# Correlation and mixing with 32x32 blocks: four tiles of the PE array in place of block-diagonal 128x128 operands

## The reference, cut to what matters

```python
x = x + xattn(layernorm(x), ctx, ctx, Wq, bq, Wk, bk, Wv, bv, Wo, bo)
x = x + ffn(layernorm(x), W_in, b_in, W_out, b_out)

# xattn
qf = jnp.fft.rfft(qt)
kf = jnp.fft.rfft(kt)
c = qf.real * kf.real + 1j * -(qf.imag * kf.imag)
corr = jnp.fft.irfft(c, n=Lq)
mean_value = jnp.mean(corr, axis=(1, 2))           # over heads and channels: 2048 delays
weights, delay = jax.lax.top_k(mean_value, top_k)  # top_k = int(2 * ln 2048) = 15
tmp_corr = softmax(weights)
out = sum_k tmp_corr[k] * roll(v, -delay[k])       # then out @ Wo + bo
```

## Time and profile before

| | |
|---|---|
| median of 3 runs | 185.46 us (182.85 to 186.11) |
| the profiled execution | 184.77 us, of it 183.0 us from the first to the last instruction |
| TensorE, DVE, ACT, GpSimd busy | 164.3, 129.0, 123.8, 30.3 us |
| from the first GR matmul to the first TR matmul | 39.87 to 91.32 us |
| granted TensorE clock, mean | 0.986 of 2.4 GHz |

### The profile page before, as it was taken

One profiled execution on the slowest core, in us unless ns is written; L12 is line 12 of the kernel. 1 busy time (PEld: TensorE's weight loads), 2 busy tenths in 40 slices (PEclk: granted clock), 3 DMA queues, 4 the chain that ended last, 5 costly groups with the idle time before them and its releaser, 6 DMA issues.

```text
span 183.0 us, 2815 instructions
## 1 busy us (share of the span) xinstructions
PE 164.3 (90%) x1054; PEld 120.7 (66%) x1054; DVE 129.0 (70%) x262; ACT 123.8 (68%) x203; POOL 30.3 (17%) x47
## 2 busy tenths in 40 slices
PE   7599999989997949999899967899999979999991
PEld 5499444979965626999756655444444547888880
DVE  1006697936456657973349978699997779999964
ACT  3254347766666993134653999999898849999910
POOL 5004000300003000000005820006920005212000
PEclk9999999999999996999999999999999999999998
DMA  4999998000000000000000000000000000001316
GB/s 142 262 290 407 441 351 274 3 0 4 2 0 4 0 0 0 0 0 0 0 4 0 2 4 0 0 0 0 4 2 0 0 0 4 0 0 61 134 38 229
DMA packets 6268, 12.17 MB, mean 66 GB/s; under 512 B 576, under 2 KB 4032, under 8 KB 6128
## 3 DMA queue, kind: packets, MB, share of 16 engines
q1 hardware_dynamic: 6112, 11.99, 19.2%
q10 hardware_dynamic: 144, 0.01, 0.1%
HBM read 9.90 MB, written 2.10 MB: 66 GB/s over the span
## 4 chain that ended last, share of the span: by engine, by line
PE 70%; ACT 14%; DVE 7%; DMA 4%; issue 3%; SPq 1%; DVEq 0%
PE ps L1184 13%; PE ps L968 8%; PE ps L1152 7%; PE ps L1157 7%; PE ps L958 6%; PE ps L991 4%; PE ps L1083 4%; PE ps L980 4%; DMA arena<-ctx_in_dram 4%; ACT arena L534 3%; PE ps L929 3%; PE ps L1097 3%; PE ps L1003 2%; PE ps L1072 2%; PE ps L1092 2%
## 5 line engine op out<-in xcount | busy, mean ns | idle before, releaser
L1184 PE MATMUL ps<-woutq,arena 128*128 128x256 f16 x256 | 28.7, 273 | 1.3 <-ACT arena L587 0.7
L1184 PEld LDWEIGHTS ps<-woutq,arena 128*128 128x128 f16 x256 | 24.7, 98 | 5.4 <-ACT arena L587 1.5
L572 ACT ACTIVATE arena<-ps,colv,sm 128x512 f32<-128x512 f32 x32 | 23.7, 783 | 2.0 <-PE ps L1157 0.5
L881 DVE SCALAR_TENSOR_TENSOR arena<-scr,sm,arena 128x1024 f16<-128x1024 int16 x16 | 21.3, 1373 | 0.0
L860 DVE TENSOR_REDUCE sm<-arena 128x1 f32<-128x1024 f32 (+1 forms) x17 | 18.9, 1148 | 2.5 <-ACT arena L572 2.5
L1152 PE MATMUL ps<-arena,winq 128*128 128x512 bf16 x64 | 18.6, 379 | 0.3 <-ACT arena L564 0.3
L1157 PE MATMUL ps<-arena,winq 128*128 128x512 bf16 x64 | 18.6, 379 | 0.0
L587 ACT ACTIVATE arena<-arena,sm 128x1024 f16<-128x1024 f32 x15 | 16.5, 1136 | 0.0
L958 PE MATMUL ps<-wvo,arena 128*128 128x256 f32 x64 | 16.3, 408 | 0.0
L958 PEld LDWEIGHTS ps<-wvo,arena 128*128 128x128 f32 x64 | 12.7, 205 | 3.2 <-issue 1.5
L968 PE MATMUL ps<-arena,wqk 128*128 128x512 f32 x32 | 14.0, 595 | 0.0
(11 more groups left out here) (215 smaller groups left out, 299.2 us busy)
## 6 DMA issues: line engine op xcount, KB each, us to landing
tabs<-tab_dram SPq DMA_DIRECT2D x1, 2416.0 KB, 17.0
arena<-x_dram SPq DMA_DIRECT2D x4, 512.0 KB, 9.2
out_dram<-arena SPq DMA_DIRECT2D x8, 256.0 KB, 2.1
arena<-ctx_in_dram SPq DMA_DIRECT2D x3, 448.0 KB, 7.9
arena<-winT_dram SPq DMA_DIRECT2D x1, 1024.0 KB, 18.4
arena<-wout_dram SPq DMA_DIRECT2D x1, 1024.0 KB, 19.6
arena<-ctx_in_dram SPq DMA_DIRECT2D x2, 224.0 KB, 3.1
arena<-wqT_dram SPq DMA_DIRECT2D x1, 256.0 KB, 8.5
```

What stands on the lines that cost most here:

```text
L572: a.activation(H[:, f, 512 * c:512 * c + 512], bank("M1", n), ACT.Gelu, bias=colv[:, 6 + f:7 + f], scale=sc1[:, f:f + 1]).then_inc(S["h_re ...
L881: v.scalar_tensor_tensor(out=part, in0=scr16[:, n % 4, :], scalar=rf[:, f:f + 1], in1=piece(Hhi, n), op0=ALU.mult, op1=ALU.subtract).then_ ...
L1184: return t.matmul(o[k // 2][:, 256 * (k % 2):256 * (k % 2) + 256], part[:, t0:t0 + 128], woutq[:, f, :], start=start, stop=stop)
```

## The change

- Every product of 32x32 blocks becomes four matmuls, one for each bin j of the group, with operands and result on 32 rows each (`quadrants`). BU, BUT and NM_ go, with the copies that filled them (L447, L486, L507, L756) and the memsets.
- GR: 4 matmuls with 32 weight columns and 32 moving columns, over all 128 channel rows, for each old one of 128 by 128; the result is already in row form, in 2 units, one emptied by ACT and one by DVE.
- UU: UT by `gram`, 32x32 each. IN: the sum over the frequency parts is done by 64 matmuls of 32x32 against P, with the factors in column 0 of `blocks`; the DVE steps L697, L701 and L703 go. ME and TM change places.
- Weights: W1 is transposed, SE (8 matmuls) puts the result onto rows, RR (64 matmuls of 32x32 by 1 column) replaces W2 and the products and sums on DVE. DVE then only scales a table XY (2 instructions), and MX is 128 matmuls of 32x32, two tables summed in PSUM.
- MIX is in row form (512 columns instead of 2048), OO is 128 matmuls with 32 rows, 128 weight columns and 32 moving columns. They rotate through four banks, and the four units of a channel half end together. The rank of the units changes: ACT has the units of j = 0 and 2, DVE those of 1 and 3, so ACT now adds both constants.
- VP is 16 units of one group instead of 8 of two; the exponentials no longer stand behind BUT copies and part of the quantisation on ACT; two of the four XD units of DVE go to ACT, and the reduction of wout on DVE comes ahead of GR.

The core of the diff:

```diff
             def gramian(i):
-                pe.wait_ge(S["qt_ready"], 5 + i)
                 o = take_bank(pe, "GR", i)
-                for m in range(4):
-                    g = 4 * i + m
+                for m in range(8):
                     for k in range(2):
-                        c0 = 2048 * k + 128 * g
-                        last = t.matmul(o[:, 128 * m:128 * m + 128], qt[:, c0:c0 + 128], xt[:, c0:c0 + 128],
-                                        start=(k == 0), stop=(k == 1))
...
+                        for j, q in quadrants():
+                            c0 = 2048 * k + 128 * (8 * i + m) + 32 * j
+                            last = t.matmul(o[q, 32 * m:32 * m + 32], qt[:, c0:c0 + 32], xt[:, c0:c0 + 32],
+                                            start=(k == 0), stop=(k == 1))
...
-                for g in range(4 * i, 4 * i + 4):
-                    last = t.matmul(bank("UU", 0)[:, 32 * g:32 * g + 32], BU[:, g, :], gram[:, g, :], start=True, stop=True)
+                pe.wait_ge(S["gram_d" if i else "gram_a"], 1)
+                for g in range(8 * i, 8 * i + 8):
+                    for j, q in quadrants():
+                        last = t.matmul(bank("UU", 0)[q, 32 * g:32 * g + 32], tb3("UT")[q, g, :], gram[q, g, :], start=True, stop=True)
...
-            done(t.matmul(o[0:NS, :], tb("J"), pr2.rearrange("p g c -> p (g c)"), start=True, stop=True))
+            for g in range(NG):
+                for j, q in quadrants():
+                    last = t.matmul(o[q, 0:NM], blocks[q, 32 * g:32 * g + 32], tb3("P")[q, g, :], start=(g == 0), stop=(g == NG - 1))
+            done(last)
...
+            pe.wait_ge(S["wT_ready"], 1)
+            o = take_bank(pe, "RR", 0)
+            for g in range(NG):
+                for j, q in quadrants():
+                    last = t.matmul(o[q, g:g + 1], tb3("UT")[q, g, :], wT[q, g:g + 1], start=True, stop=True)
+            done(last)
+            vproj(10, 11, 12)
+            for h in range(2):
+                pe.wait_ge(S["xy_ready"], h + 1)
+                o = take_bank(pe, "MX", h)
+                for m in range(8):
+                    for n in range(2):
+                        for j, q in quadrants():
+                            last = t.matmul(o[q, 32 * m:32 * m + 32], tb3("USW" if n else "U")[q, 8 * h + m, :], xy[q, n, 8 * h + m, :],
+                                            start=(n == 0), stop=(n == 1))
+                done(last)
+            vproj(13, 14, 15)
+            pe.wait_ge(S["mix_a"], 1)
+            pe.wait_ge(S["mix_d"], 1)
+            pe.wait_ge(S["vh_ready"], NG)
+            for h in range(2):
+                o = [take_bank(pe, "OO", 4 * h + j) for j in range(NJ)]
+                for g in range(NG):
+                    for j, q in quadrants():
+                        last = t.matmul(o[j][:, 32 * g:32 * g + 32], xh[q, 256 * g + 128 * h:256 * g + 128 * h + 128], MIX[q, g, :],
                                         start=True, stop=True)
-                    done(last)
+                        if g == NG - 1:
+                            done(last)
```

More of the change, by code:

```diff
@@ L58, in shape_tables @@
     P = V * (sign / D)[:, :, None, None]
[L59 to L63, removed]
+    USW, X, Y = U.copy(), V.copy(), np.zeros_like(V)
+    for m in range(0, NM, 2):
+        USW[:, m], USW[:, m + 1] = U[:, m + 1], U[:, m]
+        X[:, m + 1] = V[:, m]
+        Y[:, m], Y[:, m + 1] = V[:, m + 1], -V[:, m + 1]
+    X[0, 1], Y[0, 0:2] = V[0, 1], 0
     rows = [AF + 1 if x < TC - AF * NB else AF for x in range(NB)]
@@ L113, in build @@
         xt = slot(3)
[L114 to L117, removed]
+        blocks = slot(4, 528)
+        MIX = slot(4, 512, 1024).rearrange("p (g c) -> p g c", g=NG)
         ct = slot(5)
@@ L174, in build @@
         warm = small(2)
-        ab, mean, ex, wn, eq, pre, gone = (small(16) for _ in range(7))
-        negmx, zr, rz, eqrow, neq = (small(1) for _ in range(5))
+        mean, ex, wn, eq, pre, tie, eqe, top, wT = (small(16) for _ in range(9))
+        negmx, zr, rz, eqrow, neq, thr = (small(1) for _ in range(6))
         m16 = small(16, NB)
@@ L670, in _ @@
             v.tensor_scalar(ss1, ss1, 127.0, None, ALU.mult).then_inc(S["ss1_ready"], 1)
-            for k in range(1, 8, 2):
+            for k in XD_DVE:
                 filled(dve, "XD", k)
@@ L704, in _ @@
-            filled(dve, "ME", 0)
-            v.tensor_copy(mean, bank("ME", 0)[:, 0:NB]).then_inc(S["mean_ready"], 1)
+            v.tensor_copy(ins[:], bank("IN", 0)[:, 0:NM]).then_inc(S["ins_ready"], 1)
             filled(dve, "TM", 0)
@@ L776, in _ @@
+            vproj(10, 11, 12)
+            filled(dve, "MX", 1)
+            v.tensor_copy(MIX[:, 8:16, :], bank("MX", 1)[:, 0:256].rearrange("p (g c) -> p g c", g=8)).then_inc(S["mix_d"], 1)
+            vproj(13, 14, 15)
+            for u in range(1, 8, 2):
+                filled(dve, "OO", u)
+                v.tensor_copy(spectrum(u), bank("OO", u).rearrange("p (g b r) -> p g b r", g=NG, b=NB)).then_inc(S["os_d"], 1)
             y3 = yn.rearrange("p (b d) -> p b d", b=NB)
@@ L1057, in _ @@
             done(last)
-            pe.wait_ge(S["w1_ready"], 1)
-            o = take_bank(pe, "W2", 0)
-            done(t.matmul(o, tb("JT", NS), own, start=True, stop=True))
-            vproj(3)
-            vproj(4)
-            vproj(5)
-            def mix(*units):
-                for i in units:
-                    pe.wait_ge(S["nm_ready"], i // 2 + 1)
-                    pe.wait_ge(S["nm_a"], i // 2 + 1)
-                    o = take_bank(pe, "MX", i)
-                    for m in range(4):
-                        g = 4 * i + m
-                        last = t.matmul(o[:, 128 * m:128 * m + 128], BUT[:, g, :], NM_[:, g, :], start=True, stop=True)
-                    done(last)
@@ L1075, in attend @@
-            def attend(*units):
-                for i in units:
-                    q, h = i // 2, i % 2
-                    pe.wait_ge(S["vh_ready"], 2 * q + 2)
-                    pe.wait_ge(S["mix_ready"], q + 1)
-                    o = take_bank(pe, "OO", i)
-                    for m in range(4):
-                        g = 4 * q + m
-                        last = t.matmul(o[:, 128 * m:128 * m + 128], xh[:, 256 * g + 128 * h:256 * g + 128 * h + 128], MIX[:, g, :],
+            vproj(9)
```

324 lines of the change are left out of this document (128 added, 196 removed).

## The result

The changed kernel is no faster. Its median is 186.48 us (185.93 to 187.49, 4 runs) against 185.79 (182.85 to 186.72) of the kernel before on the same chip; the ratio is 1.0152, interval 1.0094 to 1.021, so by the ratio a slowdown of about 1.5%. The prediction took 2% for the bound of no change. The profiled execution takes 185.93 us with a span of 183.9 (before 184.77 and 183.0).

What follows compares the result with a forecast made beforehand. TensorE (busy 90%) was taken to bound most of the 51.45 us stage, chains of short steps the rest; -5.8 - 0.6 - 1.3 - 0.4 + 0.8 + 0.9 = -6.4 gave 178.4 us, 8-in-10 range 171 to 211.3.

Steps and rivals of the forecast that it cites:

- p: Pace per pair (weight load plus matmul) in GR, UU, IN, RR, MX; taken as 16 ns, 1 ns being 0.90 us.
- o: Pace per pair in OO, with 128 weight columns, over 256 pairs; taken as 28 ns, 111 without overlap.
- (a): GR and UU, before 12.07 us: 390 pairs would take 6.2 us at p = 16; -5.8 us.
- (b): UU to the first maximum, before 6.29 us: DVE steps go, but WVO, IN and BVO stand on the path; -0.6 us.
- (c): Maxima to wn, before 8.65 us: exponentials no longer wait for BUT copies and table load; wn after 7.35 us; -1.3 us.
- (d): wn to the first TR matmul, before 24.45 us: would take 24.1, including 1.7 gained by full clock; -0.4 us.
- (e): ACT loads the Sqrt table after its last OO copy, delaying the first TR copy; +0.8 us.
- (f): Changes of the array's shape lose about 0.1 us each, at some 12 borders instead of some 5; +0.9 us.
- case 2: Issue floor near 26 ns shared by all tiles, or little overlap: p 19 to 29, 181 to 190 us; chance 0.24.
- Case 4: Tile changes cost about 0.1 us, or clock falls to 1.2 GHz; 215 us with all pairs at 50 ns; chance 0.14.
- cases 1 and 4: The first: tiles overlap, p 7 to 19, 170 to 181 us, chance 0.42; the other is Case 4.
- case 3: Weight loads do not overlap between tiles: OO takes 28.4 us instead of 7.2; 199.6 to 211.3 us; chance 0.2.

Runs made afterwards that it cites:

- j_major: The changed kernel with the loop over the four tiles outermost in GR and OO, so only one tile works at a time; 225.19 us.
- oo_cols128: The changed kernel with 128 moving columns instead of 32 in every OO matmul (OO's values are then others); 182.98 us.
- hybrid: The changed kernel with GR and OO block-diagonal as before the change and VP units 13 to 15 between the MX units; 175.98 us, ratio 0.950.
- gr_block: The changed kernel with GR alone put back to 128 by 128 matmuls with diagonal copies; ratio 0.9979 to the kernel before, profiled execution 183.65 us.
- hybrid_oo_tiles: hybrid with OO alone back in tiles, with its MIX copies and owners of units; ratio 0.9961, profiled execution 184.2 us.

## Why the prediction failed

The forecast was 178.4 us, faster; it came out at 186.48, within 2% on the slow side. The unknown on which it hung most went its way, even further than forecast: p is 8.6 ns and not 16, o is 27.7 ns, and by its own formula that gives 178.4 + 0.90 x (8.6 - 16) = 171.7 us. The 14 us between this and the 185.93 of the profiled execution are what the steps left out.

By its parts, predicted and measured between the milestones above:

| step | predicted at p = 16 | at p = 8.6 | measured |
|---|---|---|---|
| (a) GR and UU, with the start 0.8 earlier | -5.8 | -8.7 | -4.0 |
| (b) UU to first maximum | -0.6 | -1.5 | +0.8 |
| (c) maxima to wn | -1.3 | -1.3 | -1.6 |
| (d) wn to first TR | -0.4 | -3.2 | +2.9 |
| (e), (f) from TR on, and shape changes | +1.7 | +1.7 | +2.8 |

**The missing step is the supply of instructions.** The prediction counted pairs but only priced the pace inside a stream. It looked for a floor on issue of 26 ns that holds for every pair (case 2). There is none: a pair takes 8.6 ns. But on the average of a long stream 27 ns a pair is just what the supply allows, so the number was right for the wrong quantity. What counts is how many instructions come in a row at this pace. In the kernel before the pairs of GR, UU and OO take 111 to 115 ns, four times what the supply asks. Cost: 3.7 us in (a), 0.4 in (b), 2.0 in (d).

**The clock was priced in one case only.** Case 4 let it fall because most of the array stands still, over all pairs, and gave 215 us; in the forecast it stayed full. It did fall, in part of the stage, and the tiles overlapped all the same: cases 1 and 4 held together, which the list of cases treated as alternatives. Cost: WVO 3.74 instead of 1.97, 1.8 in (b); OO 10.1 instead of 7.3, 2.8 in (d); from TR on 2.8, where the forecast had 0.8 for another reason (e), so 2.0 more; and UU at about 14 ns a pair instead of 8.6, 0.6 in (a). With the gaps and the forecast for p = 8.6 that makes 171.7 + 6.1 + 1.8 + 2.8 + 2.0 + 0.6 = 185.0 of the 185.93 measured; 0.9 us stay unassigned, and 0.8 more, since GR started that much earlier than forecast. Most of it lies in (d), where -3.2 + 2.0 + 2.8 makes +1.6 and 2.9 were measured. Of that, 0.7 is the way to RR, 3.7 us (62.10 to 65.80) for a forecast of 3.0: wn is done at 62.10, but VP units hold TensorE and W1 starts at 63.11. The filler that was to hide waits made one.

**A sign that was read past.** The prediction says that no transfer runs in the stage (0 to 2 GB/s). The 16 KB packets of the instruction queue run there in the kernel before too, at 41.76 and 59.13, one in each of the two windows with 2 GB/s; the changed kernel has ten between 40.09 and 82.47.

**What held.** OO's four row tiles overlap (28 ns; case 3, at 199.6 to 211.3, fell, and only j_major, which takes the turns away, shows 100 ns). Step (c), and with it the exponentials: DVE no longer waits for them. The gain of 1.7 from VP at full clock: from 65.87 to 77.93 it is 1.00. ACT's table load stands at 89.40, 1.28 us, ahead of the first TR copy, as (e) said, but in the changed kernel TensorE loses nothing by it: its eight TR matmuls at half clock last until 91.41 anyway, and the first of IV follows at 91.43. Its price shows where the clock is full, in oo_cols128:

```profile
90.62 1.13 PE L1043 MATMUL ps<-arena,tabs 128*128 128x512 f32 x2 [0.90 <-ACT arena L509]
```

The same wait was 0.24 us in the kernel before, so the load costs 0.7 there, and from the first TR matmul to the end are 92.3 us against 91.7. Against those 92.3 us the changed kernel's 94.5 are 2.2 more, the price of the half clock from TR on. The gap ahead of TR is 1.43 for a forecast of 1.9. That (f), 0.1 us at each change of shape, is real was not tried by itself.

The Trainium skill (TensorE: Matmul & The Clock Gate, Part 3), with about 4 ns between starts on different tiles, was the better guide to the overlap than the Trainium skill (TensorEngine Tiling (Array Packing), Instruction Overhead), whose 60 cycles would be an estimated 25 ns at 2.4 GHz: the traces have 8.4 to 9.1 ns in turns of four tiles and 29 on one tile. By the former alone the prediction had worked out 170 us, 16 below the 185.93 measured, and the two losses are what is missing.

**What stays open.** That the blocks of 256 are the loading of instructions by the instruction queue rests on the numbers, the packets of 16 KB and their spacing, and on their count: TensorE has 2210, 4135 and 3384 instructions in the traces of the kernel before, of the changed one and of hybrid, which are 8.6, 16.2 and 13.2 blocks of 256, and the queue moved 8, 16 and 13 packets. No kernel here changed the queue itself. Why the first fall of the clock starts is not separated: in the changed kernel it begins at 44.60, inside the gap before UU's second piece, and without the gaps (the profiled executions of gr_block and hybrid) it does not come, but those kernels also have wide GR matmuls. For the gaps speaks j_major: its GR and UU are narrow and without a gap, and the clock stays full until 56.54, right behind its first long gap, 1.84 us in IN.

## What to carry to other kernels

Small matmuls on four tiles in turn do overlap, here 3.4 times, so splitting a block-diagonal product pays where the columns of its weights shrink with it (UU and MX; GR only if its stream does not run dry). Before splitting, count the TensorE instructions that will stand in a row, an f32 matmul as four: past about 256 in 3.5 us the engine runs dry, and the cure is to put wide matmuls between them, not more overlap. Leave a product wide where the weight load stays at 128 columns and only the moving side shrinks (OO): it gains nothing even at full clock, and the thin stream lowers the clock for itself and for what follows.

## What the hardware showed that was not expected

- Pairs of 32x32 in turns of four tiles at 8.4 to 9.1 ns, against 29 ns on one tile.
- TensorE idle for 0.4 to 2.3 us inside or right behind runs of narrow matmuls, with no semaphore to wait for, each time ahead of an instruction whose number is a multiple of 256 behind the first such one, and with 3.5 to 3.9 us from one to the next in a long stream.
- The clock at 1.2 GHz in a stretch where TensorE was never idle (82.14 to 88.02, and from 76.98 on in hybrid_oo_tiles), with 32 moving columns for each 128 weight columns; with 128 moving columns at the same pace it stayed full (oo_cols128).
- At 1.2 GHz a pair of OO takes 53 ns instead of 27.7, though its weight load and not its 32 columns sets the pace (128 columns take the same 28 ns at full clock, oo_cols128): the loads slow with the clock too.
